# Softmax denominators one pair later, rotation in two parts, values last: an attention between two expert layers on one core

## What is computed

```python
qkv = x @ w_qkv.T                       # 16 heads of 64
q = q * cos + rotate_half(q) * sin + fenc
k = k * cos + rotate_half(k) * sin + fenc
attn = jax.nn.softmax(einsum('bhid,bhjd->bhij', q, k) * scale, axis=-1)
out = einsum('bhij,bhjd->bhid', attn, v)
x = x + out @ w_out.T + b_out
```

## Time and profile before

| | us |
|---|---|
| median of 3 runs | 1266.21 |
| lowest, highest | 1265.69, 1271.85 |
| the profiled execution | 1265.84 |
| its span, first to last instruction | 1264.0 |

### The profile page before, as it was taken

The page is one execution under the profiler, slowest core; times in us unless marked ns, Lnnn a source line. Parts: engine busy times, 40 slices in busy tenths (PEclk is TensorE's granted clock), DMA queues, the critical chain, the costliest instruction groups (busy, mean ns, idle before and its releaser), DMA issues.

```text
span 1264.0 us, 20948 instructions
## 1 busy us (share of the span) xinstructions
...
## 2 busy tenths in 40 slices
...
DMA packets 118677, 95.35 MB, mean 75 GB/s; under 512 B 75760, under 2 KB 85008, under 8 KB 118320
## 3 DMA queue, kind: packets, MB, share of 16 engines
...
q10 hardware_dynamic: 512, 0.26, 0.1%
...
## 4 chain that ended last, share of the span: by engine, by line
PE 85%; DVE 6%; issue 4%; ACT 2%; POOL 2%; DMA 1%; SPq 0%; ACTq 0%; DVEq 0%; POOLq 0%
PE banks L1165 17%; PE banks L1144 14%; PE banks L455 12%; PE banks L468 8%; PE banks L1083 7%; PE banks L1003 6%; PE banks L1181 5%; PE banks L1149 4%; PE banks L1190 4%; PE banks L1011 3%; PE banks L1122 1%; DVE side_turned L702 1%; PE banks L410 1%; POOL work L1438 1%; PE banks L417 1%
## 5 line engine op out<-in xcount | busy, mean ns | idle before, releaser
L1015 DVE TENSOR_REDUCE neg_max<-banks 128x2 f32<-128x1024 f32 x256 | 305.3, 1226 | 12.7 <-PE banks L1003 7.7
L1267 ACT ACTIVATE work<-banks 128x1024 f32<-128x1024 f32 x256 | 262.5, 1027 | 92.7 <-PE banks L1149 76.6
L1165 PE MATMUL banks<-work 128*64 128x512 f32 x1024 | 233.8, 598 | 0.0
L1438 POOL TENSOR_TENSOR work<-work 128x1024 f32<-128x1024 f32 x64 | 158.8, 2482 | 74.2 <-PE banks L1165 74.2
L1428 POOL TENSOR_TENSOR turn<-turn,side_turned 128x512 f32<-128x512 f32 x128 | 164.9, 1311 | 30.7 <-DMA side_turned<-side 30.7
L1422 POOL TENSOR_TENSOR turn<-turn,fenc 128x512 f32<-128x512 f32 x128 | 163.3, 1298 | 2.0 <-DVE side L1338 2.0
L1433 POOL TENSOR_TENSOR qk_l<-turn,qk_h 128x512 fp32r<-128x512 f32 x128 | 162.1, 1289 | 2.1 <-ACT qk_h L992 2.1
L1165 PEld LDWEIGHTS banks<-work 128*64 128x64 f32 x1024 | 67.8, 136 | 132.7 <-issue 110.0
L1359 DVE TENSOR_TENSOR work<-work 128x1024 f32<-128x1024 f32 x64 | 107.4, 1677 | 37.7 <-PE banks L1165 37.5
L816 POOL TENSOR_TENSOR o_raw<-o_raw,work 128x512 f32<-128x512 f32 x52 | 67.2, 1293 | 88.0 <-DVE o_raw L734 80.7
L816 POOL TENSOR_TENSOR work<-work 128x512 f32<-128x512 f32 x44 | 56.6, 1297 | 96.0 <-DVE work L734 49.6
...
## 6 DMA issues: line engine op xcount, KB each, us to landing
...
side_turned<-side SPq DMA_DIRECT2D x256, 128.0 KB, 3.1
rec_all<-rec_d SPq DMA_DIRECT2D x128, 128.0 KB, 2.9
...
den_d<-den_rows ACTq DMA_DIRECT2D x64, 4.0 KB
```

The source lines that it names most:

```text
L1015: return nc.vector.tensor_reduce(neg_max[:, g % 2, qt::DH], of, AX.X, ALU.max, negate=True)
L1165: ins = nc.tensor.matmul(o_bank(g)[OWN[h], :], v_all[:, kt, n * DH:(n + 1) * DH], pt[:, g % 2, kt, h * T:(h + 1) * T], start=(kt == 0), st ...
L1267: nc.scalar.activation(pt[:, g % 2, kt, :], S[kt].rearrange("p h q -> p (h q)"), ACT.Exp, scale=QSCALE).then_inc(s["probs"], 1)
L1438: nc.gpsimd.tensor_tensor(pt[:, g % 2, 2, :], pt[:, g % 2, 2, :], pt[:, g % 2, 3, :], ALU.add).then_inc(s["second_sum"], 1)
```

## The change

It does six things. (1) The denominators of pair p-2, not p-1, are made in period p, directly behind the product with values of pair p-1, and no longer at the period's end. (2) They go to bank 5, beside the product with values in bank 4, except for the last two pairs. (3) The quarters are multiplied with values in the order 2, 3, 0, 1; VectorE adds 2 and 3 in place (`late_sum`) and GpSimd 0 and 1 into the place of 3 once that is done (`early_sum`). (4) y of pair p-4 instead of p-3 stands ahead of the values, which are TensorE's last piece of a period. (5) `rope` is split: two instructions of half the size on the keys as soon as these are there, then two on the queries; there are four in place of two. (6) ScalarE copies the denominators behind the product with values; reciprocals, their transfers and `normalise` follow one period later, and at the seam one more of each is left over.

```diff
@@ attention
+            ORDER = (2, 3, 0, 1)
+            def den_bank(g):
+                return bank[5] if own_bank(g + 1) else W
@@ tensor: values, project_both, maxima
-                    at_least(pe, s["den_copied"], p - 1)
...
-                    project(g, K, KQ[:, K, :])
+                    project(g, K, KQ[:, K, :]).then_inc(s["k_ps"], 1)
...
                     if qt == 1:
                         pe.wait_ge(s["v_ready"], min(g + 2, B * 2 * TT))
-                        at_least(pe, s["den_copied"], g - 2)
-                        at_least(pe, s["y_done"], g - 4)
+                        at_least(pe, s["den_copied"], g - 3)
+                        at_least(pe, s["y_done"], g - 5)
...
                     if qt == 0:
                         at_least(pe, s["o_copied"], g - 2)
+                        at_least(pe, s["den_copied"], g - 3)
@@ tensor: denominators
-                    pe.wait_ge(s["v_ready"], min(p + 4, B * 2 * TT))
+                    if den_bank(g) is W:
+                        pe.wait_ge(s["v_ready"], B * 2 * TT)
+                        pe.wait_ge(s["maxes"], N * TT)
                     at_least(pe, s["den_copied"], g)
-                    pe.wait_ge(s["first_sum"], g + 1)
-                    pe.wait_ge(s["second_sum"], g + 1)
-                    for n, kt in enumerate((0, 2)):
+                    pe.wait_ge(s["late_sum"], g + 1)
+                    pe.wait_ge(s["early_sum"], g + 1)
+                    for kt in (2, 3):
@@ tensor: period
-                        for kt in range(TT):
+                        for kt in ORDER:
                             apply_v(last, kt)
+                    if exists(p - 2):
+                        denominators(p - 2, p)
...
+                    if exists(p - 4):
+                        project_out(p - 4, p)
                     if value_tile(p):
                         values(p)
-                    if exists(p - 3):
-                        project_out(p - 3, p)
                     if p == JOIN_FRONTS_AT:
                         pe.wait_ge(s["o_copied"], p)
+                        pe.wait_ge(s["den_copied"], p - 1)
                         ffn2["tensor"](pe, "fronts")
-                    if exists(last) and p != JOIN_LOGITS_AT:
-                        denominators(last, p)
@@ tensor: seam
                 elif tail == 0:
-                    project_out(N - 3, N)
+                    project_out(N - 4, N)
...
+                elif tail == 3:
+                    project_out(N - 3, N)
@@ scalar: exponentials, period
                     if kt == 0:
+                        at_least(act, s["early_sum"], g - 1)
+                    if kt == 2:
                         at_least(act, s["den_ps"], g - 1)
...
-                    if exists(p - 2):
-                        copy_den(p - 2)
                     if exists(last):
                         exponentials(last, 2)
...
                     if exists(last):
                         copy_o(last)
+                    if exists(p - 2):
+                        copy_den(p - 2)
@@ vector: rope, sums, period, seam
-                    for to, part in ((turn[:, g % 2], 0), (side[:], 1)):
-                        ins = nc.vector.tensor_tensor(to, KQ, rope_t[:, part:part + 1, :].broadcast_to([P, QK, T]), ALU.mult)
+                    for part, done in ((K, s["k_ps"]), (Q, s["qk_ps"])):
+                        dve.wait_ge(done, g + 1)
+                        nc.vector.tensor_tensor(turn[:, g % 2, part], KQ[:, part, :], rope_t[:, 0, :], ALU.mult)
+                        ins = nc.vector.tensor_tensor(side[:, part], KQ[:, part, :], rope_t[:, 1, :], ALU.mult)
                     ins.then_inc(s["roped"], 1)
...
+                def late_sum(g):
+                    dve.wait_ge(s["last_applied"], g + 1)
+                    nc.vector.tensor_tensor(pt[:, g % 2, 2, :], pt[:, g % 2, 2, :], pt[:, g % 2, 3, :],
+                                            ALU.add).then_inc(s["late_sum"], 1)
...
                     ffn2["vector"](dve, "experts")
+                    reciprocals(N - 3)
                     reciprocals(N - 2)
                     ffn2["vector"](dve, "masks")
@@ gpsimd
+                def early_sum(g):
                     pool.wait_ge(s["o_ps"], g + 1)
+                    pool.wait_ge(s["late_sum"], g + 1)
+                    nc.gpsimd.tensor_tensor(pt[:, g % 2, 3, :], pt[:, g % 2, 0, :], pt[:, g % 2, 1, :],
+                                            ALU.add).then_inc(s["early_sum"], 1)
@@ sync: seam
-                den_in(N - 2)
-                reciprocals_out(N - 2)
-                reciprocals_in(N - 2)
+                for g in (N - 3, N - 2):
+                    den_in(g)
+                    reciprocals_out(g)
+                    reciprocals_in(g)
                 den_in(N - 1)
```

70 lines of the change are left out of this document (32 added, 38 removed).

## The result

The changed kernel takes 1288.61 us (median of 5 runs, 1286.01 to 1289.84) where the kernel before takes 1266.21 (1263.82 to 1271.85, 5 runs): ratio 1.0173, 95% interval 1.0158 to 1.0188. It is slower by 22 us; the forecast was slower by 14, 1280 with a range from 1268 to 1287, so the time lies above it. The profiled execution of the change took 1287.48 us with a span of 1285.7, 21.7 more than the span before (1264.0). Lines of the code have moved by a few: the maxima are L1008, scores L1149 and L1154, product with values L1170, transpose L1127, projection L1088, values L1016, y L1197, denominators L1188 on TensorE; the residual is L1380 and VectorE's sum L1372; GpSimd's sum with the turned keys or queries is L1443.

What follows compares the result with a forecast made beforehand. TensorE's own chain was taken to bound the kernel, so only shortening its work or removing its waits pays. The terms, 0 - 4.3 + 0 + 4.9 + 4.9 + 7.2 + 2 = +14.7 us, gave 1280, range 1268 to 1287.

Steps and rivals of the forecast that it cites:

- part 3: VectorE at an ordinary boundary: the split rotation's residual ends at T+0.93, slack 0.11 before TensorE's second maxima; 0 us.
- part 2: TensorE's waits that go: 3.3 us at the denominators and 1.0 at y in periods 61 and 62; -4.3 us.
- part 6: The seam: VectorE's second inversion waits for denominators through the sync queue, and TensorE loses it all; +7.2 us, bounds +6 to +9.
- What bounds it: Whole kernel: TensorE itself is 85% of the chain; a change pays only by shortening its work or removing its waits.
- Part 1: New order on TensorE: same products, four changes of array division per pair before and after; 0 us, bounds -6 to 0.
- rival (a): On TensorE, strips of 32 follow strips of 64 without a drain; takes 6 us off, 1274; chance 0.14.
- rival (b): VectorE is late in every pair, the slack of 0.11 used up; +10 us over 50 pairs, 1290; chance 0.08.
- part 4: ScalarE where tokens are normalised, 7 places: exponentials start 0.7 us later and TensorE's scores wait; +4.9 us.
- part 5: ScalarE and VectorE where a new sequence enters, 7 places: residual 0.7 us late for TensorE's second product for maxima; +4.9 us.
- Part 7: The clock behind the seam: TensorE's idle time drops it to its lower level for some 4 us of work; +2 us.
- what would show it: The forecast's list of seven signs to look for in the new profile, such as one idle stretch of some 8 us.

## Why the prediction was right and wrong

The change came out 22 us slower where the prediction had 14, above its range. The step that failed is part 3, which followed VectorE alone and gave what lies behind the rotation no term; part 2 failed with it, and part 6 was too small.

**What bounds it: right.** The loss is all in waits of TensorE and the slow clock behind one of them.

**Part 1 (0): right.** 3.584 us from the product with values to the strips of 32, against 3.585 to the transpose: the step from 64 to 32 columns costs what any change of division costs, rival (a) falls, and the rule of the Trainium skill quoted there (TensorEngine Tiling (Array Packing), Key Properties) holds here. y got 0.17 cheaper and the values 0.17 dearer, twice the 0.08 expected, and cancelled.

**Part 2 (-4.3): half right.** The waits before period 5 went, 2.7. Those in periods 61 and 62 did not: "the denominators now cover that copy" was the step that failed, because the copy waits for GpSimd, GpSimd for VectorE, and the second layer's eight normalising instructions moved directly ahead of the exponentials. Net there it is +0.5 instead of -1.6.

**Part 3 (0): right for the ordinary pairs it was worked out for.** Residual at 1.00 behind the boundary, forecast 0.93, and no idle time behind it in them but 0.26 in one; rival (b) falls. The run with the split undone shows that the slack was as thin as said. But the step looked at VectorE alone, and this is where the missing term belongs: everything from the projection on, the rotation and with it the transfers of the turned halves, comes later in TensorE's row, while VectorE's sum keeps its place. It was written that everything there moves about 1.0 us closer to the boundary; who takes up the rotation's output was not asked. That is the unforeseen part: the transfers left 0.5 us later against VectorE's sum, GpSimd's sum was held up in 23 places instead of 4, and this cost 3.2 us of waits, most of them at y, 0.9 in the first pair behind a new sequence, and what part 2 missed; the transfers put first gave 6 back.

**Parts 4 and 5 (+4.9 each): right.** 4.6 and 5.5. All seven places of part 4 cost 0.66 (by part 4's own numbers, 594.13 less 593.34, it would be 0.8). In part 5, five places cost 0.6, one 1.5 and one 0.9. The 1.5 is the collision again, since it is 0.64 with the short sum and with the transfers put first; the 0.9 stays in both of these, and no run shows its cause. The runs with the early normalising and the early high part remove each, though the first gives a third of it to the pair behind.

**Part 6 (+7.2): right in mechanism, too small.** 8.7 (9.5 of idle time instead of 8.0): the second inversion came 7.8 us behind the first instead of 7.2, since the transfer of the denominators landed 2.4 us behind its issue instead of 1.9, and the masks' first instruction took 1.09 us where it had taken 0.22. The last is the collision once more, here with GpSimd's `normalise`, which the same round of transfers had just released: it was written that "no engine's speed matters" in this part, and 0.9 us of it were an engine's. The bound of 9 held the whole.

**Part 7 (+2): right in mechanism, low in size.** 2.7 by the filled wait, and 1.6 to 2.9 over the runs that keep the wait, so the rule of the Trainium skill quoted there (TensorE: Matmul & The Clock Gate, Part 1) agrees with the trace. The clock stayed low for 6 us of work, not 4.

In sum: -2.7 at the head, +0.5 behind period 60, +10.1 for parts 4 and 5, +3.2 for the waits not foreseen, +8.7 and +2.7 at the seam: 22.5. The span grew by 21.7; the 0.55 of the first expert layer and 0.2 of work (2.0 leave the head, 1.0 and 0.8 come back) make up the difference. Against the sum of 14.7 the 22.5 are 2.1 more for part 2, 0.3 for parts 4 and 5, 3.2 unforeseen, 1.5 for part 6, 0.7 for part 7. One point under "what would show it" was too narrow: it looked for idle time of ordinary pairs at the second maxima only, and it came at y.
